# A macaron layer on one core: feed-forward, output and value tiles and spike steps moved to other slots of the attention loop

## What is computed

```python
x = x + 0.5 * _L0_ffn_ref(_layernorm(x), W_fc, W_proj)
x = x + _L0_attn_ref(_layernorm(x), w_qkv, w_out, b_out)
x = x + 0.5 * _L0_ffn_ref(_layernorm(x), W_fc, W_proj)
...
# attention: 16 heads of 64, causal, slopes times distance added to the scores
sim = einsum('bhid,bhjd->bhij', q * SCALE, k) + rel * slopes
attn = softmax(where(causal, mask_value, sim))
out = einsum('bhij,bhjd->bhid', attn, v) ... @ w_out + b_out
...
# feed-forward: 128 -> 512 -> 128, then five spiking steps
h = square(relu(x @ W_fc.T)); y = h @ W_proj.T
mem_new = BETA * mem + y - reset * THRESHOLD      # reset = (mem > THRESHOLD)
spk = (mem_new > THRESHOLD)                        # the sum of spk over 5 steps, / 5
```

## Time and profile before

| | before |
|---|---|
| median of 3 runs | 1767.83 us |
| lowest and highest | 1766.23, 1768.95 us |
| span of the profiled execution, first to last instruction | 1764.1 us |
| granted PE clock, mean of the span | 0.984 |

### The profile page before, as it was taken

One profiled execution on the slowest core, in us unless ns is written; L12 is line 12 of the kernel. 1 busy time (PEld: TensorE's weight loads), 2 busy tenths in 40 slices (PEclk: granted clock), 3 DMA queues, 4 the chain that ended last, 5 costly groups with the idle time before them and its releaser, 6 DMA issues.

```text
span 1764.1 us, 39796 instructions
## 1 busy us (share of the span) xinstructions
PE 1676.8 (95%) x10902; PEld 1259.1 (71%) x10902; DVE 1206.1 (68%) x4272; ACT 1289.0 (73%) x3446; POOL 920.2 (52%) x1258
## 2 busy tenths in 40 slices
PE   4899999999999999999999999999999999999996
PEld 3767777677776777767777676776777677677775
DVE  6575776748777585775858768586785848767563
ACT  2687876777877787876877768687777868868781
POOL 2455554555545455545555545465454545546451
PEclk8999999999999999999999999999999999999998
DMA  2555453435434435443545434444443544434430
GB/s 73 114 109 111 85 119 75 102 82 109 101 81 107 89 84 108 92 104 76 105 93 107 96 82 107 90 87 107 90 103 78 109 95 94 102 82 101 94 82 13
DMA packets 80562, 164.80 MB, mean 93 GB/s; under 512 B 12880, under 2 KB 30928, under 8 KB 80208
## 3 DMA queue, kind: packets, MB, share of 16 engines
q1 hardware_dynamic: 80336, 162.12, 42.9%
HBM read 6.88 MB, written 4.19 MB: 6 GB/s over the span
## 4 chain that ended last, share of the span: by engine, by line
PE 69%; DVE 19%; issue 8%; POOL 2%; ACT 1%; DVEq 1%; DMA 1%; SPq 0%; POOLq 0%; ACTq 0%
PE bank L388 12%; PE bank L373 12%; PE bank L343 7%; PE bank L359 7%; PE bank L431 7%; PE bank L360 6%; PE bank L439 6%; PE bank L345 5%; PE bank L344 5%; DVE spikes L615 3%; DVE negsc L558 3%; DVE negmem L621 2%; DVE drive L618 2%; DVE xn L591 1%; DVE rsum L567 1%
## 5 line engine op out<-in xcount | busy, mean ns | idle before, releaser
L911 POOL TENSOR_TENSOR prob<-prob,rsum 128x512 f32<-128x512 f32 (+3 forms) x1024 | 731.7, 730 | 699.9 <-DVE rsum L567 699.6
L799 ACT ACTIVATE prob<-negsc,negmax 128x512 f32<-128x512 f32 (+3 forms) x1024 | 574.4, 565 | 124.2 <-DVE negmax L558 117.7
L810 ACT COPY probT<-bank 128x512 f32<-128x512 f32 x640 | 362.0, 587 | 194.5 <-PE bank L373 191.9
L558 DVE CUSTOM_DVE_ANT_0 negsc<-bank,alibi 128x512 f32<-128x512 f32 (+3 forms) x1024 | 466.2, 473 | 5.3 <-PE bank L360 5.3
L567 DVE RECIPROCAL rsum<-sums 128x1 f32<-128x1 f32 (+1 forms) x768 | 121.4, 158 | 483.3 <-PE bank L360 466.3
L373 PE MATMUL bank<-ident,prob 128*128 128x128 f32 x2560 | 373.6, 277 | 1.9 <-ACT probT L810 0.2
L359 PE MATMUL bank<-keys,queries 128*128 128x256 f32 (+2 forms) x1024 | 352.1, 355 | 23.1 <-DVE negmax L558 14.4
L388 PE MATMUL bank<-probT,vals 128*64 128x256 f32 (+3 forms) x2048 | 361.0, 453 | 0.3 <-ACT attT L817 0.3
L373 PEld LDWEIGHTS bank<-ident,prob 128*128 128x128 f32 x2560 | 296.2, 141 | 39.4 <-issue 28.6
L360 PE MATMUL bank<-keys,queries 128*128 128x256 f32 (+2 forms) x1024 | 321.2, 325 | 0.0
L359 PEld LDWEIGHTS bank<-keys,queries 128*128 128x128 f32 x1024 | 194.8, 190 | 74.6 <-DVE negmax L558 30.5
(11 more groups left out here) (82 smaller groups left out, 2246.3 us busy)
## 6 DMA issues: line engine op xcount, KB each, us to landing
queries<-queries SPq DMA_DIRECT2D x384, 256.0 KB, 3.0
keys<-k_lo SPq DMA_DIRECT2D x256, 128.0 KB, 2.4
keys<-keys SPq DMA_DIRECT2D x128, 128.0 KB, 3.7
x_in<-in_L_attn_x_dram SPq DMA_DIRECT2D x16, 256.0 KB, 2.9
out_dram<-x SPq DMA_DIRECT2D x16, 256.0 KB, 2.4
prob<-in_L_attn_w_qkv_dram SPq DMA_DIRECT2D x1, 1536.0 KB, 9.1
wo<-in_L_attn_w_out_dram SPq DMA_DIRECT2D x1, 512.0 KB, 10.7
probT<-in_L_ffn_W_fc_dram SPq DMA_DIRECT2D x1, 256.0 KB, 3.2
```

The costliest lines, as they stand in the source:

```text
L558: ins = dve.tensor_tensor_reduce(negsc[:, k % 3, col:col + WIDTH[i]], src, alibi[:, 2 * p + h, N - WIDTH[i]:N], 1.0, MASKED, ALU.add, ALU.min,
L799: ins = act.activation(prob[:, p % 2, h, PCOL[i]:PCOL[i] + WIDTH[i]], negsc[:, k % 3, col:col + WIDTH[i]], ACT.Exp, bias=negmax[:, p % 2, ...
L810: act.copy(probT[:, turn_slot(p, t), :], turn_bank[(len(TRUNS) * p + t) % 2][:, :]).then_inc(s_turned_out, 1)
L911: ins = pool.tensor_tensor(pr, pr, rsum[:, p % 2, seg:seg + 1].to_broadcast([P, WIDTH[i]]), ALU.mult)
```

## The change

The tables below change and nothing else. SIDE has the same 43 entries in a new order and in other beats, SPIKE1 starts in slot 2 beat 3 instead of slot 3 beat 0 and has lower counts in its beats, SPIKE3 starts one beat earlier, and the layer norms' steps move by one to six beats. Every line number of the kernel after is one higher than before.

```diff
--- before.py
+++ after.py
@@ -63,24 +63,25 @@
 
 
 SIDE = [
-    (0, 0, "q", 0, 0), (0, 1, "k", 0, 0), (0, 3, "v", 0, 0), (0, 4, "t1", 0, 1), (0, 4, "v", 1, 0),
-    (1, 0, "q", 0, 0), (1, 1, "k", 0, 0), (1, 2, "fc1", 0, 1), (1, 4, "fc1", 1, 1), (1, 4, "fc1", 2, 1),
-    (2, 0, "fc1", 3, 1), (2, 0, "q", 0, 0), (2, 1, "out", 0, -1), (2, 1, "out", 1, -1), (2, 2, "y1", 0, 1),
-    (2, 2, "k", 0, 0), (2, 3, "out", 2, -1), (2, 4, "y1", 1, 1), (2, 5, "v", 0, 0),
-    (3, 0, "v", 1, 0), (3, 0, "q", 0, 0), (3, 1, "k", 0, 0), (3, 2, "out", 3, -1),
-    (4, 0, "k", 0, 0), (4, 0, "q", 0, 0), (4, 2, "t3", 0, -1), (4, 3, "v", 0, 0), (4, 4, "v", 1, 0),
-    (5, 0, "q", 0, 0), (5, 1, "fc3", 0, -1), (5, 2, "k", 0, 0), (5, 4, "fc3", 1, -1), (5, 4, "fc3", 2, -1),
-    (5, 5, "fc3", 3, -1),
-    (6, 0, "q", 0, 0), (6, 1, "k", 0, 0), (6, 2, "y3", 0, -1), (6, 2, "y3", 1, -1), (6, 3, "t2", 0, 1),
-    (6, 4, "v", 0, 0), (6, 5, "v", 1, 0),
-    (7, 0, "q", 0, 1), (7, 1, "k", 0, 1),
+    (0, 0, "q", 0, 0), (0, 1, "k", 0, 0), (0, 2, "v", 0, 0), (0, 5, "v", 1, 0), (0, 5, "t1", 0, 1),
+    (1, 0, "q", 0, 0), (1, 0, "fc1", 0, 1), (1, 1, "k", 0, 0), (1, 1, "fc1", 1, 1), (1, 2, "fc1", 2, 1),
+    (1, 3, "fc1", 3, 1), (1, 5, "y1", 0, 1),
+    (2, 0, "q", 0, 0), (2, 1, "y1", 1, 1), (2, 1, "k", 0, 0), (2, 2, "out", 0, -1), (2, 3, "out", 1, -1),
+    (2, 5, "out", 2, -1),
+    (3, 0, "q", 0, 0), (3, 0, "out", 3, -1), (3, 1, "k", 0, 0), (3, 2, "v", 0, 0), (3, 3, "v", 1, 0),
+    (4, 0, "q", 0, 0), (4, 1, "k", 0, 0), (4, 2, "v", 0, 0), (4, 2, "t3", 0, -1), (4, 3, "v", 1, 0),
+    (4, 5, "fc3", 0, -1),
+    (5, 0, "q", 0, 0), (5, 0, "fc3", 1, -1), (5, 1, "k", 0, 0), (5, 2, "fc3", 2, -1), (5, 3, "fc3", 3, -1),
+    (5, 4, "t2", 0, 1), (5, 5, "y3", 0, -1),
+    (6, 0, "q", 0, 0), (6, 0, "y3", 1, -1), (6, 1, "k", 0, 0), (6, 2, "v", 0, 0),
+    (7, 0, "v", 1, 0), (7, 0, "q", 0, 1), (7, 1, "k", 0, 1),
 ]
 
-SPIKE1 = beats_from(3, 0, [2, 3, 1, 1, 0, 0, 1, 1, 1, 1, 2, 1])
-SPIKE3 = beats_from(6, 3, [1, 2, 2, 1, 2, 1, 2, 1, 2])
-LN1 = dict(stats=(0, 0), aggregate=(0, 1), rstd=(0, 1), normalise=(0, 3))
-LN2 = dict(stats=(5, 2), aggregate=(5, 3), rstd=(5, 3), normalise=(6, 1))
-LN3 = dict(stats=(3, 4), aggregate=(3, 5), rstd=(3, 5), normalise=(4, 0))
+SPIKE1 = beats_from(2, 3, [1, 1, 2, 1, 1, 0, 1, 1, 1, 0, 1, 1, 2, 1])
+SPIKE3 = beats_from(6, 2, [1, 1, 2, 1, 2, 1, 2, 1, 2, 1])
+LN1 = dict(stats=(0, 0), aggregate=(0, 1), rstd=(0, 1), normalise=(0, 2))
+LN2 = dict(stats=(4, 5), aggregate=(5, 0), rstd=(5, 0), normalise=(5, 2))
+LN3 = dict(stats=(3, 2), aggregate=(3, 3), rstd=(3, 3), normalise=(4, 0))
 
 
 def macaron_kernel(nc: bass.Bass, x, w_qkv, w_out, b_out, w_fc, w_proj, out):
```

## The result

The kernel after takes 1863.87 us (median of 4 runs, 1863.55 to 1865.55), the kernel before 1767.03 us in the same job: a ratio of 1.0551, 95% interval 1.0536 to 1.0566, some 97 us slower. The forecast was 1827 us, with a range of 1798 to 1848. In the profiled executions the spans are 1861.6 and 1764.1 us, 97.5 apart; in every single run the time stands 2.1 us above the span.

A forecast was written before the change was run, and what follows sets the result against it. PE was taken to set the pace, except at the end of slot 4 and in slot 7, where DVE does. Added 87 less 27 taken away gave +60 us, a span of 1824, so 1827 us measured; range 1798 to 1848.

The forecast's parts named there:

- k in slots 1, 3, 5 and 6, +55 and +20: k in beat 1 waits for q's bank: 1.15 us in slots 1, 3, 6 (+55), 1.25 in slot 5 (+20).
- Slots 1, 3 and 6 have no other waits to give back: Argument against the rival that PE's new waits give back part of their cost.
- t3, the v tiles, the transposes of slot 4: Slot 4: t3 waits (+7), second v tile's wait goes (-6), transposes start earlier (-4); slot 0: v waits (+3).
- t1, -13: Slot 0: PE's wait for the layer norm's result goes, 13 of 14.4 us.
- Everything else of the new table I cost at nothing: Rest of the table, POOL's squarings and ACT's copies included: 0, as those engines have 48% and 27% free.
- The keys' DMA at the start of a row, -4: PE's wait at a row's start, after slot 7, shrinks by 4 of 6.1 us.
- a spiking step leaves beats 4 and 5 of slot 6: Reason given for the 4 us less wait for the keys' DMA, despite 0.8 us more DVE work in slot 7.
- Head and tail, +2: Third fc tile waits 0.9 us for the second's relu, second y tile for a copy: +2, bounds 0 and 4.
- the jam behind slot 4: Rival: LN2's steps in slot 5 beat 0 delay PE, +15 to +30 on top, 1842 to 1857 us; chance 0.09.
- The waits give back: Rival: PE's pauses let other engines catch up, only +15 to +40, 1783 to 1808 us; chance 0.07.
- The rule: Rotating PSUM banks, taken at its word, prices the new bank waits at 0: -27 left, some 1741 us.

The follow-up runs named there:

- e5: Kernel before with slot 1's first fc tile moved from beat 2 to beat 0, between q and k: 1779.36 us, ratio 1.0087.
- e1: Kernel after with the side tile between q and k put ahead of q in slots 3, 5 and 6: 1814.53 us, ratio 1.0271.
- e13: Kernel after with k put ahead of the side tile of beat 0 in slots 3, 5 and 6: 1834.12 us, ratio 1.0379.
- e2: Kernel after with DVE's low half of the queries ahead of the beat's reciprocal and slope operation: 1837.22 us, ratio 1.0409.
- the narrow pair: Kernels after and before, each with the loop's spiking operations on 64 of 512 columns: 1818.97 and 1745.53 us.
- e11: Kernel before with t1 alone moved to slot 0 beat 5, behind the second v tile: 1766.63 us, ratio 1.000.
- e12: Kernel before with slot 4's second value tile alone moved from beat 4 to beat 5: 1774.24 us, ratio 1.0042.
- e15: Kernel after with the last norm's spiking operations moved so that slot 6 holds 7 instead of 5: 1893.48 us.

## Why the prediction was wrong in its size

The direction and the main term were right; the forecast had 60 of the 97 us. By its own steps:

- *k in slots 1, 3, 5 and 6, +55 and +20.* Right. Measured 1.13 us each (forecast 1.15), also in slot 5 (forecast 1.25, DVE had caught up): 64 x 1.13 = 72 of the 75 us. e5, e1, e13, e2 and the narrow pair show it from five sides. "Slots 1, 3 and 6 have no other waits to give back" held as well.
- *t3, the v tiles, the transposes of slot 4.* Right: t3 waits 0.59 (forecast 0.5), v in slot 0 0.25 (0.2), the second v tile of slot 4 had 0.50 (0.43) to lose and the transposes 0.27 (0.29). Slot 4 came to -0.30 against -0.22.
- *t1, -13.* In slot 0 right (-0.70 a row against -0.73). But e11 shows that in the kernel before the same step is worth nothing, as slot 1 takes it back, and in the kernel after slot 1 is just where 1.16 us more than forecast stand, 0.43 of them the wait for t1's low half. To take its 13 us as a gain on the span was a mistake in kind: what it freed was paid at the next thing that comes at its own time.
- *The failed step: "Everything else of the new table I cost at nothing. POOL's squarings and ACT's copies move with their tiles and those engines have 48% and 27% of the span free".* A share of the span says nothing of the beat. ACT has its 30% free elsewhere; in slot 7 the copy stood behind an exponential that was itself late, for 1.04 us in 14 rows, and in slot 1 PE waited 0.50 a row for the other copy. Beside ACT's copies the same step left out DVE's low half of t1, for which the fc tile in slot 1 waits 0.43; the 0.23 us a row that are left of slot 1's excess I can't assign. The forecast had seen the value tile come into slot 7, but only as 0.8 us more for DVE, not as a bank and a copy. I had read the order of banks for the k tiles and not for every tile of the table. The same view would have given all three: which reader must free the bank, and what that reader's engine has ahead of it.
- *The keys' DMA at the start of a row, -4.* Wrong in sign. It grew from 6.1 to 13.4 us, and the row's first score tile waits 1.76 us instead of 1.62. The reason I gave ("a spiking step leaves beats 4 and 5 of slot 6") counted operations where what DVE carries into slot 7 was the matter; how much of the longer wait is due to the added value tile no run separates.

Together the last two leave slots 1 and 7 at +1.16 and +1.48 us a row above the forecast, 14 x 2.64 = 37 us; the other slots were 0.29 a row below it (-4). Outside rows 1 to 14 the forecast had 12 us and 16 came. 60 + 37 - 4 + 5 = 98.

- *Head and tail, +2.* The head gained 2.3 us and the tail lost 4.1. In the tail the bank order does what I said and more:

```profile
1837.16 0.80 PE L344 MATMUL bank<-xf_hi,wfc_hi 128*128 128x512 f32 x1 [0.69 <-ACT hid L853]
1838.85 0.60 ACT L853 ACTIVATE hid<-bank 128x512 f32<-128x512 f32 x1 [1.74 <-PE bank L346]
1839.50 0.79 PE L344 MATMUL bank<-xf_hi,wfc_hi 128*128 128x512 f32 x1 [0.69 <-ACT hid L853]
```

The third fc tile starts 2.34 us after the second; in the kernel before it followed 1.44 us after (1743.68 to 1745.12, the latter in the earlier trace rows). That is the 0.9 forecast. The first matmuls of a tile take 0.80 and 0.79 us here, as the one after the jump back in the earlier trace rows.

**The rivals.** The range reached to 1848 for the jam behind slot 4. It did not come: t3 and slot 5 were as forecast. A jam of that size did come, but behind slots 6 and 0, at ACT's copies. "The waits give back" had no part in the four bank waits: e1 took two of them and part of a third away, worth 42 us, and 49 us came back.

**The rule.** The forecast weighed a page of the Trainium skill (Perfetto Trace Analysis, Matmuls) that wants independent groups of matmuls to rotate through different PSUM banks. The kernel after rotates two, and the four turns whose reader has a slope operation ahead of it cost 1.13 us each: the trace does not bear out a price of nothing. What the Trainium skill (Perfetto Trace Analysis, Optimization Strategy) says of consistent bubbles fits: the same 1.13 us in four slots of rows 1 to 15. That more banks would cure it was not tried.

**Open.** The 24 us that depend on DVE's load stand mostly in slot 7, by the narrow pair, but are not split by cause: every kernel that removed one wait there brought another, so there is no share for each. e12's 7 us are placed, in the landing of one transfer in half of the rows; why that takes longer is open.

## What to carry to other kernels

When tiles share a few banks in turn, write for every tile of the new order who frees its bank and what that engine has ahead of the freeing operation; the wait is that end less PE's own work in between, and here it could be read from the old trace to 0.02 us. A share of free time over the span is no cover: look at the beat. And a wait that is removed is worth nothing until the next thing that arrives at its own time (here a chain of four transfers, or DVE's backlog) has been looked up behind it. A new wait can cost more than its length: behind pauses of over 2 us PE ran at a lower clock in most rows of e2 and e15.
